# Routed gates and adding gathers in a fused attention and mixture-of-experts layer

## The reference

```python
s1 = where(causal, einsum('bhqd,bhkd->bhqk', q, k1) * SCALE, MIN)      # the same for s2 with k2
attn = softmax(s1) - sigmoid(lambda_logit) * softmax(s2)
attn = attn / maximum(sum(abs(attn), -1), 1e-6)
x = layernorm(x + (attn @ v) @ Wo.T)

xn = layernorm(x) * gamma + beta                                        # B x T x D = 8 x 512 x 128
w, idx = top_k(softmax(xn @ router_w.T / 1.5), 2)                       # of E = 8 experts
h = silu(xn @ W1[e]);  y = h @ W2[e]                                    # hidden width 512
x = layernorm(x + sum over the two experts of w * y)
```

## Time and profile before

| | |
|---|---|
| median of 3 runs | 1152.73 us (1149.02 to 1153.8) |
| profiled execution | 1139.17 us, span 1137.3 us |
| granted TensorE clock, mean | 0.877 |
| busy: TensorE products, weight loads | 908.5 us (80%), 726.7 us (64%) |
| busy: VectorE | 935.6 us (82%) |
| busy: ScalarE | 841.1 us (74%) |
| busy: GpSimd | 846.0 us (74%) |

### The profile page before, as it was taken

How to read it: one execution, slowest core, us unless ns; L and a number is a source line. 1 busy time by engine, 2 the same in 40 slices (tenths; PEclk the granted TensorE clock), 3 DMA queues, 4 the chain that set the end, 5 groups by cost and what they waited for, 6 DMA issues and landing times. The chain is left out here.

```text
span 1137.3 us, 27887 instructions
## 1 busy us (share of the span) xinstructions
PE 908.5 (80%) x8522; PEld 726.7 (64%) x8522; DVE 935.6 (82%) x2425; ACT 841.1 (74%) x2706; POOL 846.0 (74%) x1144
## 2 busy tenths in 40 slices
PE   2487877879889788978889778978889888978681
PEld 1255555657678576766677566767677676768571
DVE  0499998889998899899999899889999899955132
ACT  1499988688887788788888788787888778853130
POOL 3389978788778888698778988798878986781503
PEclk9579788778998899889999899889999799988696
DMA  3703400533246623482237523582237523246562
GB/s 100 177 10 98 108 1 16 140 100 117 84 122 176 182 76 108 132 246 88 75 122 186 174 74 108 156 238 71 77 120 198 154 73 113 87 147 198 172 215 61
DMA packets 117045, 139.38 MB, mean 123 GB/s; under 512 B 11042, under 2 KB 99490, under 8 KB 116898
## 3 DMA queue, kind: packets, MB, share of 16 engines
q1 hardware_dynamic: 112802, 129.21, 38.3%
q0 software_dynamic: 4096, 8.40, 2.6%
HBM read 107.81 MB, written 29.75 MB: 121 GB/s over the span
## 5 line engine op out<-in xcount | busy, mean ns | idle before, releaser
L700 ACT ACTIVATE exps<-scores,neg_max 128x512 f32<-128x512 f32 (+3 forms) x1024 | 542.9, 551 | 102.1 <-DVE neg_max L989 101.1
L989 DVE TENSOR_REDUCE neg_max<-scores 128x1 f32<-128x512 f32 (+3 forms) x896 | 423.4, 524 | 51.3 <-PE scores L1119 49.1
L627 POOL TENSOR_TENSOR exps<-exps 128x512 f32<-128x512 f32 x256 | 326.7, 1276 | 21.4
L623 POOL TENSOR_SCALAR exps<-exps,inv_l,lam_l 128x384 f32<-128x384 f32 (+3 forms) x448 | 272.7, 615 | 87.2 <-DVE inv_l L964 75.6
L1151 PE MATMUL trans<-ident,exps 128*128 128x128 f32 x1280 | 234.6, 313 | 91.3 <-ACT diffT L707 69.3
L1117 PE MATMUL scores<-stack 72*128 72x512 bf16 (+3 forms) x1024 | 272.6, 335 | 16.6 <-DMA stack<-parts_dram 15.6
L1151 PEld LDWEIGHTS trans<-ident,exps 128*128 128x128 f32 x1280 | 158.4, 158 | 155.3 <-issue 95.3
L700 ACT ACTIVATION_READ_ACCUMULATOR exps<-scores,neg_max 128x1 f32 x1024 | 235.8, 230 | 0.0
L999 DVE TENSOR_REDUCE abs_sum<-exps 128x1 f32<-128x512 f32 (+3 forms) x448 | 222.8, 520 | 8.8 <-POOL exps L627 8.8
L707 ACT ACTIVATE diffT<-trans 128x512 f32<-128x512 f32 x320 | 196.4, 614 | 35.1 <-PE trans L1151 34.3
L1119 PE MATMUL scores<-causal_bf,ident_bf 128*128 128x128 bf16 x1024 | 209.0, 237 | 0.0
(11 more groups left out here) (138 smaller groups left out, 921.6 us busy)
## 6 DMA issues: line engine op xcount, KB each, us to landing
w_sb<-w_dram SPq DMA_DIRECT2D x120, 512.0 KB, 3.8
stack<-parts_dram SPq DMA_DIRECT2D x288, 96.0 KB
parts_dram<-parts SPq DMA_DIRECT2D x104, 128.0 KB
xg<-x_sorted_dram SPq DMA_DIRECT2D x24, 256.0 KB, 4.2
y_sorted_dram<-y_sorted SPq DMA_DIRECT2D x24, 256.0 KB, 4.5
x_in<-x_dram SPq DMA_DIRECT2D x8, 256.0 KB, 4.7
x_res<-x_dram SPq DMA_DIRECT2D x8, 256.0 KB, 4.8
o_dram<-y_out SPq DMA_DIRECT2D x8, 256.0 KB, 2.3
```

What stands on the lines that cost most here:

```text
L623: nc.gpsimd.tensor_scalar(diff[:, ring, col:col + w], exps[:, ring, 1, col:col + w], inv_l2[:, i:i + 1], lam_l1[:, i:i + 1], ALU.mult, ALU ...
L627: nc.gpsimd.tensor_tensor(diff[:, ring, :], diff[:, ring, :], exps[:, ring, 0, :], ALU.subtract)\
L700: nc.scalar.activation(exps[:, ring, k, col:col + w], scores[:, c % 2, k, col:col + w], ACT.Exp, bias=neg_max[:, c % 2, k, i:i + 1], accum ...
L989: nc.vector.tensor_reduce(neg_max[:, c % 2, k, i:i + many], scores[:, c % 2, k, col:col + many * w].rearrange("p (i w) -> p i w", w=w), AX ...
```

## The change

- **Gates ride with the rows.** `xh` becomes two copies of the normalised rows with 129 columns; the last routing step writes each row's two gates into column 128 of the two copies instead of `gates`. ScalarE makes the second copy of the rows. Scatters write rows of 129 values, the sorted loads bring them, and ScalarE multiplies by the gate when it copies an expert's output.
- **Transfers add.** The gathers write into `x1_twice` (now three buffers) with an add instead of into `y_back`; gathers 4 to 7 wait for gathers 0 to 3. The `combine` tasks are gone, as are `y_back`, `acc` and `gates`; `norm3` waits for the last four gathers.
- **Value copies** go from VectorE to GpSimd, at the same slot 8.
- **Masks**: one product with the identity adds the mask to both units of a chunk.
- **Late weights**: in the last batch tiles 4 to 14 get buffers of their own in the rings `exps` and `diffT`, which are free then. The first weights task issues loads 0 to 4, the third one loads 5 to 14.
- **Lags**: eight exponential buffers, transposes, their copies, weighted sums and absolute sums one slot later. The last weighted sum of a batch then stands at slot 9 of the next body.
- **Slots** of `den_T`, one weights, one turn, the scatters, one gather and one prep task move by one or two. The last expert copy of the batch before has to be done before `sorted`.

```diff
-LAG_TRANS = 5
+LAG_TRANS = 6
-LAG_ABS = 5
+LAG_ABS = 6
-EXP_RING, DIFF_RING = 7, 12
+EXP_RING, DIFF_RING = 8, 12
...
-SCATTER_SLOTS = (31, 32, 32, 34, 34, 35, 36, 37)
-GATHER_SLOTS = (82, 83, 85, 85, 87, 88, 88, 90)
-COMBINE_SLOTS = (86, 86, 88, 90, 91, 91, 91, 93)
+SCATTER_SLOTS = (31, 31, 31, 33, 33, 34, 35, 36)
+GATHER_SLOTS = (82, 83, 85, 85, 85, 88, 88, 90)
+LATE_SLOT = next(j for j, slot in enumerate(WEIGHT_SLOTS) if slot > POST_SLOTS["sorted"])
+LATE = TILES - WEIGHTS_AHEAD
+LATE_FIRST = 5
...
+            def load_weights(n, j):
+                i = n * TILES + j
+                if not late(n, j):
+                    m, used = divmod(i - WEIGHTS_AHEAD, TILES)
+                    sp.wait_ge(expert_psum.sem, expert_psum.after(m, psum_count[("post", "expert", used)]))
+                    loaded = weights_loaded[i % WEIGHTS_AHEAD].sem
+                else:
...
+                    sp.wait_ge(pv_done.sem, pv_done.after(n, NG * NT))
+                    loaded = late_loaded[j - WEIGHTS_AHEAD]
...
                 if name == "sorted":
                     sp.wait_ge(scattered.sem, scattered.after(n, TOP * NT))
-                    sp.wait_ge(turned.sem, turned.after(n - 1, len(CHUNKS)))
+                    sp.wait_ge(y_copied.sem, y_copied.after(n - 1, TILES))
...
+                    if slot == V_SLOT and "attention" in stages:
+
+                        pool.wait_ge(v_evacuated.sem, v_evacuated.after(b, 1))
+                        pool.wait_ge(pv_done.sem, pv_done.after(b - 1, NG * NT))
+                        for g in range(NG):
+                            last = nc.gpsimd.tensor_copy(
...
+                            if i >= NT:
+                                pool.wait_ge(gathered[i - NT].sem, gathered[i - NT].after(n, 1))
                             nc.gpsimd.indirect_dma_start(
-                                y_back[:, i, :], None, y_dram[n % 2][:, :],
-                                bass.IndirectOffsetOnAxis(ap=place_int[:, n % 2, i:i + 1], axis=0)).then_inc(gathered[i].sem, 16)
+                                x1_twice[:, n % 3, i % NT, :], None, y_dram[n % 2][:, :],
+                                bass.IndirectOffsetOnAxis(ap=place_int[:, n % 2, i:i + 1], axis=0),
+                                compute_op=ALU.add).then_inc(gathered[i].sem, 16)
...
+                            act.wait_ge(xh_done.sem, xh_done.after(n, 1))
+                            nc.scalar.activation(xh[:, 1, :, 0:D], xh[:, 0, :, 0:D], ACT.Copy).then_inc(xh_copied.sem, 1)
...
-                            nc.scalar.activation(y_sorted[:, c % 2, j % NT, :], bank[:, 0:D], ACT.Copy)\
+                            nc.scalar.activation(y_sorted[:, c % 2, j % NT, :], bank[:, 0:D], ACT.Copy, scale=xg[:, j, D:D + 1])\
...
-                    i = nc.vector.tensor_scalar(gates[:, n % 2, :, :], top[:, :, :], 0.5, None, ALU.mult)
+                    i = nc.vector.tensor_scalar(xh[:, :, :, D], top[:, :, :], 0.5, None, ALU.mult)
...
-                                last = nc.tensor.matmul(scores[:, c % 2, k, col + w - P:col + w], ident_bf[:, :],
-                                                        causal_bf[:, :], start=False, stop=True)
...
+                            last = nc.tensor.matmul(blocks[:, ends[0]:ends[-1] + 1:step, :], ident_bf[:, :],
+                                                    causal_bf[:, :].unsqueeze(1).broadcast_to([P, len(ends), P]),
+                                                    start=False, stop=True, skip_group_check=True)
```

## The result

The changed kernel takes 1156.12 us (median of 20 runs, 1150.65 to 1164.48) where the kernel before takes 1148.84 us (20 runs, 1142.73 to 1156.29) beside it: ratio 1.0058, 95% interval 1.0037 to 1.0078. It is slower by 0.6%, where 3% faster was forecast. Its profiled run has a span of 1149.1 us, 11.8 more than the one of before; that is more than the 7 us between the medians, because the profiled run of before (1139.17 us) is faster than any of the 20.

A forecast was written before the change was run, and what follows sets the result against it. VectorE, 92 to 93% busy, was taken to bound the bodies, and a chain the tail. Bodies -27 and tail -7.5 gave -34.5 us, ratio 0.970, so 1118 us; range 1100 to 1141.

The forecast's parts named there:

- Hidden by that room: 0: Attention bodies: GpSimd's queue some 3 us later after taking the value copies; transposes and sums, one slot later, absorb it, costing 0.
- Combines off VectorE: Bodies 3 to 7: removing eight combines frees 3.7 us each, 18.5 us together, seven eighths counted as wall time.
- Value copies: All eight bodies: moving them off VectorE frees 0.84 us each, 6.7 us, seven eighths as wall time; GpSimd's cost hidden.
- Lags: Attention bodies: earlier scatters, later transposes and sums, ring of eight take 5 us of VectorE's 22.5 us waiting for scores.
- Masks: Attention bodies, TensorE: 640 mask products instead of 1024 and 384 fewer weight loads; 1 us gained, bounds 0 and 42.
- Rows of 516 bytes: Scatters and sorted loads: longer rows cost 0 to 1 us a load, inside the slot of room.
- Adding gathers: GpSimd: issue stays at 1.02 us, landing 1 us later than 3.3; bounds were today's values and twice both.
- rival (d): Bodies and tail: an adding gather costs GpSimd twice, eight more us per body; 1141 us, chance 0.07.
- Rival (e): GpSimd stands at gathers 4 to 7 because adding gathers land late, deciding near 12 us; about 1203 us, chance 0.07.
- Rival (a): Attention bodies: VectorE's freed time becomes waiting for scores, half of 25.2 us stays; 1132 us, chance 0.20.
- the forecast's own signs of being wrong: VectorE's score waits grow by what it was freed of, gather issue near 2 us, or GpSimd's value-copy wait delays transposes.
- Tail: After the last chunk: late weights -9 us, loads queued ahead +1 (0 to 3), end with adding gathers +0.5; -7.5 us.

## Why the prediction was wrong

The step that failed most is the one about GpSimd: "Who waits for that: transposes and sums ... Hidden by that room: 0", with today's issue time for an adding gather. In its place GpSimd's added load doubled VectorE's normalisations in slot 17 (11.1 to 22.2 us, slot 17 +13.6), the adding gathers cost 7.4 us, and the lag that was to give the room and 5 us more cost 8 with what moves with it. In the tail the price of the queue order and of the gathers, put at 1.5 us, was 8.

- **Combines off VectorE: right, a little too high.** 18.5 us, of which seven eighths as wall time (16), measured alone 13.1 us.
- **Value copies: sign right, size wrong.** The cost on GpSimd was small as assumed (0.29 us each, 1.16 a body), but VectorE's 6.7 us weren't won: with the copies back on VectorE the time is the same within the noise. The step "Hidden by that room: 0" failed in that the room is itself bought.
- **Lags: wrong in sign.** -5 was taken, +8 measured for lags, ring and slots without the rest. VectorE's wait for scores did fall by 4 and the transposes' by 5.4. But the wait for the sorted rows, which the moved scatters were to remove, rose from 11.7 to 20.7 us, and slots 5, 10 and 30 grew. I costed the waits that the moves remove and not what they put elsewhere; why it is 8 us in all stays open.
- **Masks:** -1 forecast, -3 measured.
- **Rows of 516 bytes: right for the loads, blind for the prologue.** "0 to 1 us a load, inside the room above" holds: the loads are no slower. But rows of 516 bytes cost 5.3 us of time, 4.4 of them in the prologue, which the forecast did not look at though the same buffers are cleared there.
- **Adding gathers: the bound chosen at the wrong end.** Issue 1.02 (today's) was taken with twice as the other end; it is 1.56. This is half of rival (d), put at 7%. Its sentence by the Trainium skill ("Collectives: The Full Stack", "The bandwidth ceiling: the fold count and why AG ≠ RS ≠ AR"), that by that rule the landing grows and not GpSimd's issue, is only half of it: the landing grew by 0.9 us, as far as the traces have landings, and the issue by half. Rival (e) was far off: the longest landing in the trace was 6.8 us and the point of decision 12, and gathers 4 to 7 stood for an earlier one only twice, for 1.5 us together.
- **GpSimd's load on VectorE: missing.** The forecast asked who waits for a later GpSimd, and answered: transposes and sums, which have room. It didn't ask which VectorE instructions had been running beside an idle GpSimd. It named the exclusion of the two engines for the combines, which go, and for the copies against VectorE's coefficient step; the normalisations, 11.1 us in ten groups, it did not name, and they doubled. Rival (a), freed time becomes waiting, came true in part: VectorE's wait for scores rose from 22.5 to 32.3 us. That is one of the forecast's own signs of being wrong, at 10 of the 25 us.
- **Tail: gain nearly right, price wrong.** The tiles took 29.6 in place of 36.5 us with late weights alone, 29 to 31 in the changed kernel's variants and 33.1 in its own profile; the forecast was 9 us. "+1 (0 to 3)" for the loads ahead was 3 to 5: the third load waits for a buffer, with late weights alone until after the scatter, and the sorted rows share the transfers with the others. The end took 4.8 us more for eight adding gathers, where 8 was the far bound. So the tail is 4.9 us longer in the profiles, where -7.5 was forecast.

Summed, the single parts give: combines -13.1, masks -3.3, late weights -2, lags and slots +8.3, rows +5.3, adding +7.4 (undone in the changed kernel): +2.6 us, where +6.7 was measured. Each part is known to 2 to 4 us, so the sum is good to about 8 us (an estimate from the intervals) and what it leaves needs no cause. That parts do interact is shown by single runs: the lag costs time on the kernel before and saves it in the changed one.

## What to carry to other kernels

When work moves from the bound engine to one at 75% busy, look where that engine stands idle now, and what the bound engine does there: time that looks free may be what keeps two engines out of each other's way. Cost every property of a transfer that changes (row length, where rows start, plain or adding) as a change of its own, in the prologue too. Put loads that may wait for a buffer behind the load that the path needs: here that order was worth 2 to 5 us, and late weights in that order with the joint masks take 0.6% less than the kernel before (1142.9 us). And look which transfers a landing time belongs to before you build on it: two clearing stores at the start passed here for 32 loads.

## What the runs showed of the hardware

- An indirect transfer that adds in fp32 costs GpSimd 1.56 us for 128 rows, one that overwrites 0.96 to 1.02.
- Two stores of 128 x 15 rows from SBUF, one behind the other, landed in 5.0 and 8.3 us with rows of 512 bytes, in 8.0 and 12.9 with rows of 516 end to end, in 5.5 and 9.1 with 516 on a pitch of 1024, in 5.3 and 8.9 with rows of 576. Loads of such rows back into SBUF were no slower at 516 bytes (5.9 us from issue to use against 6.2). The Trainium skill, "DMA: Bandwidth & Descriptors", section "How a descriptor splits into AXI transactions", gives a row that doesn't start at a multiple of 256 bytes some extra beats. By its counting a row of 516 bytes takes 17 beats in place of 16 when it starts at such a multiple and, as an estimate, about 21 on average when it doesn't, so at most 1.3 times. Measured for the stores are 1.1 times on the pitch of 1024 and 1.5 to 1.6 times end to end: the first is near its counting, the second above it. The loads show none of it.
- A fp32 normalisation of 128x128 on VectorE, 0.34 us alone, takes up to 1.37 us beside a subtraction of 128x512 on GpSimd, and the subtraction 1.40 in place of 1.27. Wholly inside a scaling (`tensor_scalar`) on GpSimd 16 of them took 0.33 to 0.34 us. Additions of 128x512 on VectorE take 1.05 in place of 0.68 us beside such a subtraction.
